# Selection stored as a plain 128x128 block and spread over groups by a mask on VectorE

## The reference, cut to what matters

```python
grouped = x.reshape(B, S // 16, 16, D)                        # groups of 16 rows (tokens)
cont_logits = einsum('bgtd,des->bgtes', grouped, controller) + tie
cont_perm = (cont_logits == max(cont_logits, axis=t))         # 0/1: which token a slot takes
inner = relu(einsum('bgtesf,bgtes->bgesf', intermediate, cont_perm))
inter2 = einsum('bgesf,esfd->bgesd', inner, f2)
result = einsum('bgesd,bgtes->bgtd', inter2, cont_perm)       # back to the tokens
x = x + result
```

## Time and profile before

| what | value |
|---|---|
| median of 3 runs | 1958.4 us (1956.91 to 1960.88) |
| the profiled execution, its own time | 1965.0 us |
| its span, first to last instruction | 1963.3 us |
| PE busy | 1824.5 us (93%) |
| DVE busy | 1170.8 us (60%) |
| ACT busy | 988.4 us (50%) |
| POOL busy | 356.6 us (18%) |
| mean granted TensorE clock | 0.970 |

### The profile page before, as it was taken

How to read it: one execution, slowest core, us unless ns; L and a number is a source line. 1 busy time by engine, 2 the same in 40 slices (tenths; PEclk the granted TensorE clock), 3 DMA queues, 4 the chain that set the end, 5 groups by cost and what they waited for, 6 DMA issues and landing times. The chain is left out here.

```text
span 1963.3 us, 40727 instructions
## 1 busy us (share of the span) xinstructions
PE 1824.5 (93%) x15580; PEld 1320.5 (67%) x15580; DVE 1170.8 (60%) x2339; ACT 988.4 (50%) x1716; POOL 356.6 (18%) x387
## 2 busy tenths in 40 slices
PE   5487699999999989999999977999999999999999
PEld 3344578888888878888888866555555565665554
DVE  6488466666666544333333336767767777777665
ACT  2355123333333366556655524766657667666653
POOL 4476220000000000000000024222223223222210
PEclk9787899999999999999999989999999999999999
DMA  9987755566666374334433357555546555556433
GB/s 368 301 163 107 169 168 167 167 177 183 180 179 179 122 275 149 126 127 162 150 125 125 116 163 242 161 156 176 163 150 196 154 164 180 164 171 181 136 111 114
DMA packets 246960, 332.09 MB, mean 169 GB/s; under 512 B 58049, under 2 KB 170177, under 8 KB 243618
## 3 DMA queue, kind: packets, MB, share of 16 engines
q1 hardware_dynamic: 237855, 309.11, 50.4%
q0 software_dynamic: 8960, 20.98, 5.6%
HBM read 189.43 MB, written 140.61 MB: 168 GB/s over the span
## 5 line engine op out<-in xcount | busy, mean ns | idle before, releaser
L1535 PE MATMUL bank<-f2s,inner_bd 128*32 128x512 f32 x2528 | 295.8, 598 | 0.6 <-issue 0.4
L599 ACT ACTIVATE h1o<-bank,b_by_channel 128x500 f32<-128x500 f32 x160 | 108.5, 678 | 324.6 <-PE bank L431 316.1
L1434 ACT ACTIVATE inter_hi<-bank 128x512 fp32r<-128x512 f32 x316 | 189.2, 599 | 162.6 <-PE bank L1535 161.6
L1356 DVE TENSOR_TENSOR inter_lo<-bank,inter_hi 128x512 fp32r<-128x512 f32 x316 | 216.2, 689 | 68.0 <-ACT inter_hi L1434 63.2
L429 PE MATMUL bank<-hhi,w_hi 128*128 128x500 f32 x624 | 244.5, 392 | 0.0
L431 PE MATMUL bank<-hhi,w_lo 128*128 128x500 f32 x624 | 243.5, 390 | 0.0
L430 PE MATMUL bank<-hlo,w_hi 128*128 128x500 f32 x624 | 242.6, 389 | 0.0
L429 PE MATMUL bank<-ahi,w_hi 128*128 128x500 f32 x608 | 237.3, 390 | 0.0
L430 PE MATMUL bank<-alo,w_hi 128*128 128x500 f32 x608 | 236.6, 389 | 0.0
L431 PE MATMUL bank<-ahi,w_lo 128*128 128x500 f32 x608 | 236.4, 389 | 0.0
L563 DVE BATCH_NORM_STATS2 stats<-h1o 128x500 f32 (+1 forms) x160 | 103.2, 674 | 155.5 <-ACT h1o L599 155.5
(11 more groups left out here) (140 smaller groups left out, 3240.7 us busy)
## 6 DMA issues: line engine op xcount, KB each, us to landing
h1T<-h1o SPq DMA_DIRECT2D x19, 2000.0 KB, 8.1
h1in<-h1T SPq DMA_DIRECT2D x19, 2000.0 KB, 9.7
aggregate<-at SPq DMA_DIRECT2D x20, 1024.0 KB, 8.9
x<-in_x SPq DMA_DIRECT2D x79, 256.0 KB, 3.2
x<-x SPq DMA_DIRECT2D x79, 256.0 KB, 3.6
back_f<-selection SPq DMA_DIRECT2D x79, 256.0 KB, 3.2
x_back<-x SPq DMA_DIRECT2D x79, 256.0 KB, 3.3
out<-x_back SPq DMA_DIRECT2D x79, 256.0 KB, 2.2
```

Of the source, the lines that this page charges most:

```text
L599: nc.scalar.activation(h1o[b][:, m, :], mb[m % 4][:, 0:CW], ACT.Identity, bias=b1c[:, m:m + 1]).then_inc(evr, 1)
L1356: nc.vector.tensor_tensor(ilo[b][:, :], bI[b][:, :], ihi[b][:, :].bitcast(F32), ALU.subtract).then_inc(ilr, 1)
L1434: nc.scalar.activation(ihi[b][:, :], bI[b][:, :], ACT.Copy).then_inc(ihr, 1)
L1535: last = nc.tensor.matmul(bI[b][32 * i:32 * i + 32, :], ibd[:, e, j, :, :].rearrange("p s g -> p (s g)"), f2s[:, e, :], start=True, stop=True)
```

## The change

The tensor in DRAM becomes [6, 128, 128], and a pair is stored in it as it stands, one run of 512 bytes for each partition. The load picks out for partition (q, g) the 16 tokens of group g, in 64-byte runs, for both tiles of a pair in one DMA: 8 runs a partition, 64 KB. Nothing is zeroed any more. The zeros come from DVE: `back_rows` multiplies the 16 loaded tokens, read 8 times over, by a mask of (partition, group). The mask is made once.

```diff
-        rbf = [sb(f"back_f{i}", [P, QB, P]) for i in range(2)]
+        rbf = [sb(f"back_f{i}", [P, 2 * QB, GT]) for i in range(2)]
...
-                    if static(q, 1):
-                        sp.wait_ge(zf, 16 * SLOTS)
-                    if not static(q, SLOTS // 2):
-                        for i in range(2):
-                            sp.wait_ge(lds[i], 16 * (q - SLOTS // 2 + 1))
-                    slot = q % (SLOTS // 2) * 2 * ES * GB * P
-                    sp.dma_start(bass.AP(seld.tensor, slot, [[GB * P, n], [P + GT, GB], [1, GT]]),
-                                 pn[q % 2][0:n, :].bitcast(F32).rearrange("p (g t) -> p g t", t=GT)).then_inc(sst[q % 2], 16)
+                    if not static(q, SLOTS):
+                        sp.wait_ge(lds[q % 2], 16 * (q // 2 - SLOTS // 2 + 1))
+                    sp.dma_start(seld[q % SLOTS, 0:n, :], pn[q % 2][0:n, :].bitcast(F32)).then_inc(sst[q % 2], 16)
...
-                    if not static(t, 2):
-                        sp.wait_ge(rr, t - 1)
-                    sp.dma_start(rbf[t % 2][:, :, :], seld[t % SLOTS].rearrange("(b q) g t -> (q g) b t", b=QB))\
-                        .then_inc(lds[t % 2], 16)
+                    if not static(q, 2):
+                        sp.wait_ge(rr, 2 * q - 2)
+                    sp.dma_start(rbf[q % 2][:, 0:n * QB, :],
+                                 bass.AP(seld.tensor, q % SLOTS * P * P, [[GT, P], [GT * P, n * QB], [1, GT]]))\
+                        .then_inc(lds[q % 2], 16)
...
-                        sp.wait_ge(szr, 1)
-                        for i in range(SLOTS):
-                            sp.dma_start(seld[i].rearrange("e g t -> (e g t)").rearrange("(p n) -> p n", p=P),
-                                         x1b[0][:, :]).then_inc(zf, 16)
...
-                            for ahead in range(t if t == 0 else t + 1, min(t + 2, NT)):
-                                load_selection(ahead)
+                            if kb == 0 and n == 0:
+                                load_selection(0, 0)
+                            if n % 2 == 0 and exists(kb, n + 2):
+                                load_selection((kb * TB + n + 2) // TB, (n + 2) % TB // 2)
...
-                nc.gpsimd.memset(x1b[0][:, :], 0.0).then_inc(szr, 1)
...
+                    nc.vector.tensor_scalar(pq[:, 1:2], pidx[:, :], GB - 1, None, ALU.bitwise_and).then_inc(cstv, 1)
...
+                    nc.vector.tensor_scalar(mrg[:, :], gid[:, :], pqf[:, 1:2], None, ALU.is_equal).then_inc(cstv, 1)
...
-                    nc.vector.tensor_copy(rbd[j % 2][:, :, :], rbf[j % 2][:, :, :]).then_inc(rr, 1)
+                    nc.vector.tensor_tensor(rbd[j % 2][:, :, :].rearrange("p b (g t) -> p b g t", t=GT),
+                                            rbf[q % 2][:, i * QB:(i + 1) * QB, :].unsqueeze(2).to_broadcast([P, QB, GB, GT]),
+                                            mrg[:, :].unsqueeze(1).unsqueeze(3).to_broadcast([P, QB, GB, GT]),
+                                            ALU.mult).then_inc(rr, 1)
```

More of the change, by code:

```diff
@@ L42 @@
 GH = GB // 2
-SLOTS = 12
+SLOTS = 6
 HP = P // 2
@@ L895, in mixture @@
         eye = sb("eye", [P, P], F32R)
-        pidx, pq = sb("pidx", [P, 1], I32), sb("pq", [P, 1], I32)
-        pqf = sb("pqf", [P, 1])
+        pidx, pq = sb("pidx", [P, 1], I32), sb("pq", [P, 2], I32)
+        pqf = sb("pqf", [P, 2])
         gid = sb("gid", [P, GB])
-        mtg = sb("mask_token_group", [P, GH])
+        mtg, mrg = sb("mask_token_group", [P, GH]), sb("mask_row_group", [P, GB])
         bA, bB, bD, bI = psum[0], psum[1], psum[2:4], psum[4:8]
@@ L920, in mixture @@
         lgp, lgr, mxr = sem("logits_psum"), sem("logits_ready"), sem("max_ready")
-        zf, szr = sem("selection_zeroed"), sem("zero_rows_ready")
         sst = [sem(f"selection_stored{i}") for i in range(2)]
@@ L927, in mixture @@
         fp, otr = sem("final_psum"), sem("out_ready")
-        CONSTA = GT + 4
+        CONSTA, CONSTV = GT + 5, GT + 6
         CONSTP = 2
@@ L1182, in store_selection, with load_selection @@
                     sp.wait_ge(pnr, q + 1)
[L1183 to L1199 removed]
+                    if not static(q, SLOTS):
+                        sp.wait_ge(lds[q % 2], 16 * (q // 2 - SLOTS // 2 + 1))
+                    sp.dma_start(seld[q % SLOTS, 0:n, :], pn[q % 2][0:n, :].bitcast(F32)).then_inc(sst[q % 2], 16)
+                def load_selection(kb, p):
+                    q, n = kb * (TB // 2) + p, pair_size(kb, p)
+                    sp.wait_ge(sst[q % 2], 16 * (q // 2 + 1))
+                    if not static(q, 2):
[3 more added lines that the diff above has]
+                        .then_inc(lds[q % 2], 16)
                 def store_out(kb, j):
@@ L1287, in constants @@
                         .then_inc(cstv, 1)
-                    dve.wait_ge(cstv, GT + 2)
-                    nc.vector.tensor_copy(pqf[:, 0:1], pq[:, 0:1]).then_inc(cstv, 1)
+                    nc.vector.tensor_scalar(pq[:, 1:2], pidx[:, :], GB - 1, None, ALU.bitwise_and).then_inc(cstv, 1)
                     dve.wait_ge(cstv, GT + 3)
+                    nc.vector.tensor_copy(pqf[:, :], pq[:, :]).then_inc(cstv, 1)
+                    dve.wait_ge(cstv, GT + 4)
                     nc.vector.tensor_scalar(mtg[:, :], gid[:, 0:GH], pqf[:, 0:1], None, ALU.is_equal).then_inc(cstv, 1)
+                    nc.vector.tensor_scalar(mrg[:, :], gid[:, :], pqf[:, 1:2], None, ALU.is_equal).then_inc(cstv, 1)
                 def new_tile(k, j):
@@ L1345, in back_rows @@
                     t = kb * TB + j
-                    dve.wait_ge(lds[j % 2], by2(t, j % 2, 16))
+                    q, i = t // 2, t % 2
+                    if static(t, 1):
+                        dve.wait_ge(cstv, CONSTV)
+                    dve.wait_ge(lds[q % 2], 16 * (q // 2 + 1))
                     if not static(t, 2):
                         dve.wait_ge(fp, (t - 1) * QB)
-                    nc.vector.tensor_copy(rbd[j % 2][:, :, :], rbf[j % 2][:, :, :]).then_inc(rr, 1)
+                    nc.vector.tensor_tensor(rbd[j % 2][:, :, :].rearrange("p b (g t) -> p b g t", t=GT),
+                                            rbf[q % 2][:, i * QB:(i + 1) * QB, :].unsqueeze(2).to_broadcast([P, QB, GB, GT]),
+                                            mrg[:, :].unsqueeze(1).unsqueeze(3).to_broadcast([P, QB, GB, GT]),
+                                            ALU.mult).then_inc(rr, 1)
                 def inter_low(kb, u):
@@ L1611, in gnn_mixture @@
     x1d = nc.dram_tensor("x1", [NB * BW, H], F32, kind="Internal").ap()
-    seld = nc.dram_tensor("selection", [SLOTS, ES, GB, P], F32, kind="Internal").ap()
+    seld = nc.dram_tensor("selection", [SLOTS, P, P], F32, kind="Internal").ap()
     with ExitStack() as ctx:
```

1 line of the change is left out of this document (removed).

## The result

| | before | after |
|---|---|---|
| timed, us (median; lowest to highest of 4) | 1958.76; 1956.91 to 1960.88 | 1946.94; 1945.12 to 1950.37 |
| ratio, with its 95% interval | 1 | 0.9936 [0.9924, 0.9949] |
| profiled execution: span; its own time | 1963.3; 1965.0 | 1948.7; 1950.37 |
| PE busy in the stretch of the earlier trace rows | 194.63 of 200 | 195.91 of 200 |
| packets; MB moved | 246960; 332.09 | 209215; 310.81 |

The account below looks back on a forecast made before the run. PE was taken to bound the kernel from the first back half on, DMA waits the first block. Start -5.3 us, back halves on DVE 0, DMA and SP 0: 1953.1 us against the median, range 1949.5 to 1957.5.

Parts of the forecast that it names:

- What bounds the kernel, the start: First block: without the zeroing, tile 0 is stored earlier and x loads through the buffer ring come earlier, -5.6 us.
- The new constants: DVE before the first normalisation: two more instructions and one twice as wide cost 0.3 us, between 0 and 0.46.
- The sum of -5.3: Start of the mixture: -5.6 us from earlier tiles plus 0.3 us for added DVE instructions; bounds -2.8 and about -8.
- Rival (a): First block: the lead is partly given back, only tile 2's 2.84 us less 0.3 remain, 1955.9 us; chance 0.19.
- Rival (c): First block: selection stores in long runs let x stores land sooner, -8.1 us in all, 1950.3 us; chance 0.08.
- The back halves on DVE: 0: Back halves: 79 copies become products, 0.27 us longer each, 21.5 us more DVE work, hidden by idle time: 0 us.
- the cover: Back halves: DVE idle time hiding the longer product, 0.63 us in tiles without `spread`, 0.38 us in tiles with it.
- Rival (b): Back halves: the DVE product meets POOL's `xn_lo` and delays PE; with 0.3 us in 40 tiles, 1965 us; chance 0.10.
- DMA and SP: Back halves: smaller selection loads and 40 fewer SP issues change nothing, since PE waits nowhere for these DMAs: 0 us.

Follow-up runs that it names:

- k1: The kernel before with its twelve zeroing DMAs moved some 440 us ahead, into an earlier stage; ratio 0.9976, 1957.31 us for 1961.61.
- k2: The changed kernel with twelve zeroing DMAs and their wait put back, into a tensor nobody reads; ratio 0.9989 to the kernel before.
- k4: The changed kernel with selection stores in 64-byte runs again, loads strided to match; ratio 0.9960 to the kernel before, 1953.42 us for 1961.61.
- k3: The kernel before with DVE's copy to `back_bd` made a product of the same input by itself; ratio 1.0002.
- k5: The changed kernel plus a 192 KB load for each back-half tile that nobody reads; ratio 0.9973 to the kernel before, 1956.87 us.
- k11: The changed kernel plus a 192 KB load that nobody reads, only at tile 0 of each block; ratio 0.9960 to the kernel before.
- k6: The changed kernel loading only 16 of 512 columns of `x_back` from the third tile on; ratio 0.9949 to the kernel before.

## Why the prediction was right in direction and short in size

**What bounds the kernel, the start.** Right, nearly step by step. Forecast and measured: store of tile 0 at 1154.1 and 1153.81; tile 2 at 1164.15 and 1164.22, with no wait; tile 3 at 1167.2 and 1167.16; tile 4 at 1171.2 and 1171.25. One detail was wrong and cost nothing: tile 4 waits 0.48 us for PE, since the store of tile 2 was followed by the next load after 2.5 us and not 3.5. The new constants cost some 0.2 us (`xn` at 1156.02 for 1156.04, with x0 0.23 us earlier), forecast 0.3. The sum of -5.3 stands against a mean of -5.1 over three traces, -5.7 if only the first block is taken. The three scatter over 2.8 us, so that the sum came out so near is partly luck. Rival (a), the lead given back, did not come about; k1 and k2 show that it hangs on the zeroing. Rival (c) can't be told (k4).

**The back halves on DVE: 0.** Right. k3 alone gives 1.0002, and the cover was where the rows had it. Rival (b) needed `xn_lo` to come first, and it never did in the tiles read.

**DMA and SP: "PE waits nowhere for these DMAs: 0".** This is the step that failed; it measured -6.1 us on average over the traces, with 717.5 us of back halves for heavy loads and 711.4 for light ones. I asked only whether someone waits for the data of the shrunken loads. Nobody does. But instruction packets go through the same 16 DMA engines (the profile counts q8 in their share), and, as inferred above, PE waits for these. What a whole stretch shows: from the second to the last `back_bd` the windows give, before and after,

```profile
1235.10:1954.97 719.87, 701.47 (x9939) 415.39 (x9935) 510.41 (x1012) 455.99 (x860) 167.27 (x203) 1.00 0.54 161
```

```profile
1228.77:1940.37 711.60, 696.85 (x9939) 414.54 (x9935) 526.99 (x1012) 456.30 (x860) 173.62 (x203) 1.00 0.47 138
```

PE's idle time is 18.4 us before and 14.8 after, its busy time 4.6 us longer for the same 9939 matmuls. Both parts of the 8.3 us are there: longer stops, and slower products. The five traces with heavy loads have 16.9 to 18.9 us idle and 698.9 to 701.5 busy, the other nine 14.2 to 15.3 and 695.6 to 698.1. The list of PE's waits in the same stretches has it by the line of the short products (total, times, longest), before and after:

```profile
PE bank L1571 <- issue: 9.5, 10, 1.9
```

```profile
PE bank L1570 <- issue: 6.1, 8, 1.2
```

Row 1's 194.63 of 200 us should have made me ask what the other 5.4 are. I took PE to be the bound and its idle time to be none of the change's business; a list of PE's waits with the releaser "issue" would have shown 9.5 us that nothing in the sum accounted for (3.4 of them went), and a change that takes 21 MB off the DMA engines next to it.

The Trainium skill, Runtime: NRT & Kernel Launch, section "Instruction fetch mechanics", says that instructions come in blocks of 16 KiB through a DMA queue of the engine's own, and that the cost of crossing a block is mostly hidden. The packets of 16 KB agree. Mostly hidden holds too for 15580 matmuls at large, but not for 128 short products in a row: at the third crossing the stop is 0.8 to 1.4 us with light loads ahead of it, and 1.1 to 2.2 us with the 256 KB load or 192 KB added.

**What stays open.** That traffic makes the difference is shown in the traces (k5, k11, the three traces of the changed kernel, k6 as the end of it), and that it acts at the crossings by the distances. The times bear it out in direction, with 3.4 us for k5 and, for k11, a loss that is smaller than in its trace, if it is one. That the delayed instruction packet is the way in which it acts rests on its position in 14 traces, on the stop's fixed place in PE's program and on "issue" as the releaser; no experiment moved the packet alone, for instance by shifting the code by some instructions. What fills the 2.3 to 2.9 us from the packet to PE's next product I don't know. Between before and after, the stops and the lower clock name the whole of the step at the eighth crossing (0.6 us) and most of it at the third and fourth (2.4 of 2.8, 1.3 of 1.6). At the second, 0.7 of the 1.4 us is idle time of PE and the other 0.7 busy time; at the fifth the whole 1.0 us is busy time, 25.90 against 24.90 us for the same 659 matmuls, with a granted clock of 1.00 in both (the crossing before, then after):

```profile
1597.26:1623.92 26.66, 25.90 (x659) 16.68 (x661) 17.17 (x35) 14.91 (x30) 6.31 (x7) 1.00 0.46 140
```

```profile
1585.12:1610.77 25.65, 24.90 (x659) 16.64 (x661) 17.57 (x35) 14.93 (x30) 6.53 (x8) 1.00 0.41 124
```

What slows PE's products there these traces don't show.

## What to carry to other kernels

For each DMA that a change shrinks or adds, ask two questions: who waits for its data, and what else stands in the same DMA engines, PE's instructions among them. A bound engine with idle time put down to "issue" in a run of short matmuls may be open to such traffic. Here ten loads of 192 KB just ahead of such runs brought some 6 us in one trace, and moving the last small loads away from there brought nothing that is shown. Follow a queue's blockage through the ring buffer, instruction by instruction; this gave the start to within 0.1 us at three of four places and to 0.3 us at the other.

## What was unexpected of the hardware

- A run of 128 products of 64 columns (some 2.2 us without its pause) stops after 96 products in all 14 traces: for 0.84 to 1.40 us with light loads ahead (nine kernels), for 1.13 to 1.94 with a load of 256 KB (before, k1, k3) and 2.20 and 2.22 with 192 KB added (k5, k11).
- After the stop of 1.93 us the granted clock was 0.83 over the next 10 us and 16 long products took 3.50 us for 1.92. k3 repeats this: a stop of 1.94 us, then 0.83 and 3.43 us. After the stops of 2.20 and 2.22 us in k5 and k11 it stayed at 1.00. What decides it these runs don't show.
- Twelve issues of 256 KB in a row hold SP for 8.5 us, 0.7 each; the single issues of that size in the first block take 0.33 to 0.72.
